# Four graph networks on 1,250 nodes: edge lists loaded ahead of x, rows moved as 120 and 5, last network's logits on TensorE and its residual inside the last head

## The reference

```python
hv = h.reshape(n, H, DIN)                       # H = 12, DIN = DOUT = 64
ft = jnp.einsum('nhd,od->nho', hv, W)
a1 = jnp.sum(ft * attn_l, axis=-1)
a2 = jnp.sum(ft * attn_r, axis=-1)
e = jax.nn.leaky_relu(a1[src] + a2[dst], negative_slope=0.2)
m = jax.ops.segment_max(e, dst, num_segments=n)
w = jnp.exp(e - m[dst])
alpha = w / jnp.maximum(segment_sum(w, dst)[dst], 1e-16)
agg = jax.ops.segment_sum(alpha[:, :, None] * ft[src], dst, num_segments=n)
res = jnp.einsum('nhd,od->nho', hv, W_res)
out = jax.nn.relu((agg + res).reshape(n, H * DOUT))
x = _layernorm(x + out, axis=-1)
```

## Time and profile before

| | us |
|---|---|
| three runs | 3564.36 (median), 3555.25, 3577.82 |
| the profiled execution | 3568.32 |
| its span, first to last instruction | 3566.5 |
| mean granted clock of TensorE | 0.944 of full |
| start to the end of the counting stage | 0 to 366 |
| first network | 366 to 1258 |
| second network | 1258 to 2770 |
| third network | 2770 to 2980 |
| last network: projections | 2980 to 3045 |
| last network: heads | 3045 to 3511 |
| tail and stores | 3511 to 3566.5 |

### The profile page before, as it was taken

How to read it: one execution, slowest core, us unless ns; L and a number is a source line. 1 busy time by engine, 2 the same in 40 slices (tenths; PEclk the granted TensorE clock), 3 DMA queues, 4 the chain that set the end, 5 groups by cost and what they waited for, 6 DMA issues and landing times. The chain is left out here.

```text
span 3566.5 us, 60526 instructions
## 1 busy us (share of the span) xinstructions
PE 3236.0 (91%) x20691; PEld 3023.4 (85%) x20691; DVE 2210.2 (62%) x4068; ACT 1338.6 (38%) x2524; POOL 930.8 (26%) x967
## 2 busy tenths in 40 slices
PE   3997997999998999999999899999989897899993
PEld 3886776888888999999988899999978585799993
DVE  3888736667677531118878401258868348888895
ACT  1145223333323121124546211134454212677782
POOL 1100733444445430014546200035555000000000
PEclk9988998999999999999999999999999798899896
DMA  2023433122111244247767433367766201000001
GB/s 78 23 79 94 141 112 107 55 97 90 58 61 62 92 129 129 90 142 244 240 207 241 151 113 101 100 202 241 238 202 191 89 22 72 1 1 1 0 1 44
DMA packets 157898, 386.93 MB, mean 108 GB/s; under 512 B 27083, under 2 KB 96248, under 8 KB 157673
## 3 DMA queue, kind: packets, MB, share of 16 engines
q0 software_dynamic: 47200, 173.39, 15.9%
q1 hardware_dynamic: 72989, 147.94, 11.9%
q10 hardware_dynamic: 37484, 62.75, 5.6%
HBM read 284.69 MB, written 99.32 MB: 108 GB/s over the span
## 5 line engine op out<-in xcount | busy, mean ns | idle before, releaser
L1832 PE MATMUL bank<-w_hi,xT_hi 128*125 128x384 f32 x1920 | 653.1, 340 | 8.0 <-ACT arena L1536 8.0
L1833 PE MATMUL bank<-w_lo,xT_hi 128*125 128x384 f32 x1920 | 650.9, 339 | 0.0
L1834 PE MATMUL bank<-w_hi,xT_lo 128*125 128x384 f32 x1920 | 650.8, 339 | 0.0
L1536 ACT COPY arena<-bank 125x384 f32<-125x384 f32 x320 | 153.6, 480 | 800.1 <-PE bank L1834 746.1
L817 POOL DMA_INDIRECT arena<-y_early,edges x204 | 233.9, 1146 | 817.3 <-issue 362.8
L891 DVE SCALAR_TENSOR_TENSOR row_lo<-arena,edges,row_hi 128x768 fp32r<-128x768 f32 x300 | 304.1, 1014 | 120.9 <-ACT row_hi L860 81.4
L2299 DVE CAST w_hi<-w_raw 128x2304 fp32r<-128x2304 f32 x35 | 47.6, 1359 | 531.4 <-PE bank L1834 525.5
L1832 PEld LDWEIGHTS bank<-w_hi,xT_hi 128*125 128x125 f32 x1920 | 358.3, 187 | 8.9 <-DVE w_lo L2300 4.7
L1833 PEld LDWEIGHTS bank<-w_lo,xT_hi 128*125 128x125 f32 x1920 | 358.3, 187 | 0.1
L1834 PEld LDWEIGHTS bank<-w_hi,xT_lo 128*125 128x125 f32 x1920 | 358.0, 186 | 0.1
L730 ACT ACTIVATE arena<-arena,low 125x1250 f32<-125x1250 f32 x170 | 227.7, 1339 | 345.0 <-DVE low L742 344.3
(11 more groups left out here) (351 smaller groups left out, 6628.7 us busy)
## 6 DMA issues: line engine op xcount, KB each, us to landing
y_early<-arena SPq DMA_DIRECT2D x200, 187.5 KB
w_raw<-in_L_gnn_W_dram ACTq DMA_DIRECT2D x30, 1152.0 KB, 7.4
arena<-own_mask_d SPq DMA_DIRECT2D x50, 610.4 KB
y_late<-arena SPq DMA_DIRECT2D x120, 187.5 KB
h_d<-arena ACTq DMA_DIRECT2D x40, 250.0 KB
arena<-in_L_gnn_W_dram SPq DMA_DIRECT2D x5, 1536.0 KB, 10.6
arena<-h_d ACTq DMA_DIRECT2D x30, 250.0 KB
wadj_d<-arena SPq DMA_DIRECT2D x10, 625.0 KB
```

Of the source, the lines that this page charges most:

```text
L1832: pe.matmul(b, xT_hi[:, k, v], w_hi[:, h, k], start=(k == 0), stop=False)
L1833: pe.matmul(b, xT_hi[:, k, v], w_lo[:, h, k], start=False, stop=False)
L1834: ins = pe.matmul(b, xT_lo[:, k, v], w_hi[:, h, k], start=False, stop=(k == KD - 1))
```

## The change

It has four parts. SP issues the twelve edge loads first and the load of x behind them. Loads and stores with 125 rows outermost are issued in two pieces, rows 0 to 119 and rows 120 to 124 (ROWS): the load of x, load_h, load_mask, the mask of the last network and the output stores; waits on their semaphores count two DMAs. Other transfers of 125 rows keep their form. In the last network's projection stage the attention vectors are laid out by chunk of 128 input columns (att3, 24 columns), multiplied once by the weights into logit3, and TensorE then computes logits with a 4-column matmul beside each 256-column one, all into bank 7, from which VectorE copies them to al3 at the end; its products and reductions go. In the last head, VectorE adds the residual and takes the statistics of a tile as soon as the tile's last head is in, computes the moments of the first seven tiles (ENDS = NT - 3) behind unit 16 of the pair, and normalises them behind unit 17; the last three follow after the last unit. ScalarE's square root is split the same way.

```diff
+        att3 = cut(at, KD, 2, 2)
+        logit3 = cut(at + 4 * KD, KD, 2, 2)
+        ENDS = NT - 3
...
+        ROWS = ((0, P - P % 15), (P - P % 15, P))
...
-            sp.dma_start(node_a, a["x"].rearrange("(n p) d -> p n d", p=P)).then_inc(bulk_loaded, 16)
-
             sp.wait_ge(rows_ready, 1)
             for i, v in enumerate([a["dst"], a["src"], a["edge_type_8"], a["edge_weight"]]):
...
+            for lo, hi in ROWS:
+                sp.dma_start(node_a[lo:hi], a["x"].rearrange("(n p) d -> p n d", p=P)[lo:hi]).then_inc(bulk_loaded, 16)
...
             def load_h(h):
-                sp.dma_start(h_raw[h % 2], h_d[h].rearrange("(n p) c -> p n c", p=P)).then_inc(h_loaded, 16)
+                for lo, hi in ROWS:
+                    sp.dma_start(h_raw[h % 2][lo:hi], h_d[h].rearrange("(n p) c -> p n c", p=P)[lo:hi]).then_inc(h_loaded, 16)
...
-                sp.dma_start(mask_slot[u % 2], own_mask_d[u % NT * P:(u % NT + 1) * P, :]).then_inc(mask_in[u % 2], 16)
+                for lo, hi in ROWS:
+                    sp.dma_start(mask_slot[u % 2][lo:hi], own_mask_d[u % NT * P + lo:u % NT * P + hi, :]).then_inc(mask_in[u % 2], 16)
...
-            sp.dma_start(att3[:, 0], spread(a["L3_gnn_attn_l"][0].rearrange("h c -> (h c)"), P)).then_inc(w3_loaded, 16)
-            sp.dma_start(att3[:, 1], spread(a["L3_gnn_attn_r"][0].rearrange("h c -> (h c)"), P)).then_inc(w3_loaded, 16)
-            sp.wait_ge(w3_cleared, 1)
+            sp.wait_ge(w3_cleared, 2)
+            for i, v in enumerate((a["L3_gnn_attn_l"], a["L3_gnn_attn_r"])):
+                for q in range(2):
+                    sp.dma_start(att3[q * C3:(q + 1) * C3, :, i, q], v[0].rearrange("(k q) c -> q c k", q=2)[q],
+                                 allow_slow_non_contiguous=True).then_inc(w3_loaded, 16)
...
-            sp.dma_start(mask, mask_d.rearrange("(n p) s -> p n s", p=P)).then_inc(mask_loaded, 16)
+            for lo, hi in ROWS:
+                sp.dma_start(mask[lo:hi], mask_d.rearrange("(n p) s -> p n s", p=P)[lo:hi]).then_inc(mask_loaded, 16)
...
-                sp.dma_start(out[d * P:(d + 1) * P, :], node_b[:, d]).then_inc(x_saved[d % 2], 16)
+                for (lo, hi), stored in zip(ROWS, x_saved):
+                    sp.dma_start(out[d * P + lo:d * P + hi, :], node_b[lo:hi, d]).then_inc(stored, 16)
...
+            act.copy(logit3.rearrange("p k i q -> p (k i q)"), bank[7][:, 0:4 * KD]).then_inc(w3T_ready, 1)
             act.copy(w3T.rearrange("p a b -> p (a b)"), bank[6][:, 0:256]).then_inc(w3T_ready, 1)
...
+                    if last and k == PAIR - 3:
+                        act_sqrt(act, "sqrt_act", rstd[:, 0:ENDS])
...
+            pe.matmul(bank[7][:, 0:4 * KD], w3[:, 0], att3.rearrange("p k i q -> p (k i q)"), start=True, stop=True).then_inc(w3_turned, 1)
+            pe.wait_ge(w3T_ready, 2)
...
                     for c in range(2):
-                        ins = pe.matmul(bank[q % 6][0:P, c * 256:(c + 1) * 256], xT[:, 2 * g + c, n * P:(n + 1) * P],
+                        k = 2 * g + c
+                        pe.matmul(bank[7][0:P, 4 * (n * KD + k):4 * (n * KD + k + 1)], xT[:, k, n * P:(n + 1) * P],
+                                  logit3[:, k].rearrange("p i q -> p (i q)"), start=True, stop=True)
+                        ins = pe.matmul(bank[q % 6][0:P, c * 256:(c + 1) * 256], xT[:, k, n * P:(n + 1) * P],
...
-                dve.wait_ge(f_taken, 3 * (n + 1))
-                for i in range(2):
-                    chain(dve.tensor_tensor(scratch3, node_a[:, n], att3[:, i], op=ALU.mult))
-                    chain(dve.tensor_reduce(al3[:, i, n], scratch3.rearrange("p (h c) -> p h c", c=C3), axis=AX_X, op=ALU.add))
+            for i in range(2):
+                chain.mark(dve.tensor_copy(al3[:, i].rearrange("p n (k q) -> p n k q", q=2),
+                                           bank[7][0:P, 0:4 * KD * NT].rearrange("p (n k i q) -> p n k i q", n=NT, k=KD, i=2)[:, :, :, i]))
...
+                    if last and q:
+                        dve.wait_ge(agg_taken, unit(u + k))
+                        chain(dve.scalar_tensor_tensor(node_b[:, d], res3[:, d], 0.0, node_b[:, d], op0=ALU.max, op1=ALU.add))
+                        dve_stats(dve, chain, node_b, d)
+                        if d == ENDS - 1:
+                            dve_moments(dve, chain, range(ENDS))
+                        if d == ENDS:
+                            dve_scale(dve, chain, node_b, node_b, range(ENDS))
```

More of the change, by code:

```diff
@@ L348, in build @@
         al3 = cut(rest + NT * N + node, 2, NT, H3, parts=P)
-        att3 = cut(rest + NT * N + node + 2 * NT * H3, 2, D, parts=P)
+        at = rest + NT * N + node + 2 * NT * H3
+        att3 = cut(at, KD, 2, 2)
+        logit3 = cut(at + 4 * KD, KD, 2, 2)
+        ENDS = NT - 3
         w3 = cut(rest + NT * N + node + 2 * NT * H3 + 2 * D, 2, 128)
         w3T = cut(rest + NT * N + node + 2 * NT * H3 + 2 * D + 256, 2, 128)
-        scratch3 = cut(rest + NT * N + node + 2 * NT * H3 + 2 * D + 512, D, parts=P)
         s_row3 = cut(rest + NT * N + node + 2 * NT * H3, 2, N, parts=P)
@@ L1153, in _ @@
                 sp.wait_ge(ln_done, 3 * NT + d + 1)
-                sp.dma_start(out[d * P:(d + 1) * P, :], node_b[:, d]).then_inc(x_saved[d % 2], 16)
-            for i in range(2):
-                sp.wait_ge(x_saved[i], 16 * NT)
+                for (lo, hi), stored in zip(ROWS, x_saved):
+                    sp.dma_start(out[d * P + lo:d * P + hi, :], node_b[lo:hi, d]).then_inc(stored, 16)
+            for stored in x_saved:
+                sp.wait_ge(stored, 16 * NT // 2 + 16 * NT)
         @block.gpsimd
@@ L1342, in _ @@
             next_phase(pool)
+            pool.memset(att3, 0.0).then_inc(w3_cleared, 1)
             pool.memset(w3, 0.0).then_inc(w3_cleared, 1)
@@ L1642, in _ @@
             act_pair(H3 // 2 - 1, True)
[L1643 removed]
+            act_sqrt(act, "sqrt_act", rstd[:, ENDS:NT])
         @block.tensor
@@ L2376, in _ @@
             next_phase(dve)
-            dve.wait_ge(bulk_loaded, 16 * 7)
+            dve.wait_ge(bulk_loaded, 16 * 8)
             for n in range(NT):
@@ L2425, in _ @@
             next_phase(dve)
-            dve.wait_ge(bulk_loaded, 16 * 9)
+            dve.wait_ge(bulk_loaded, 16 * 10)
             for n in range(NT):
@@ L2445, in _ @@
                                     bank[q % 6][0:P, :].rearrange("p (c i f) -> p c i f", c=2, i=2)[:, :, 0]).then_inc(f_taken, 1)
-                dve.wait_ge(f_taken, 3 * (n + 1))
-                for i in range(2):
-                    chain(dve.tensor_tensor(scratch3, node_a[:, n], att3[:, i], op=ALU.mult))
-                    chain(dve.tensor_reduce(al3[:, i, n], scratch3.rearrange("p (h c) -> p h c", c=C3), axis=AX_X, op=ALU.add))
+            for i in range(2):
+                chain.mark(dve.tensor_copy(al3[:, i].rearrange("p n (k q) -> p n k q", q=2),
+                                           bank[7][0:P, 0:4 * KD * NT].rearrange("p (n k i q) -> p n k i q", n=NT, k=KD, i=2)[:, :, :, i]))
             next_phase(dve)
-            dve.wait_ge(mask_loaded, 16)
+            dve.wait_ge(mask_loaded, 32)
             chain(dve.tensor_scalar(al3[:, 1], al3[:, 1], SLOPE - 1.0, None, op0=ALU.mult))
@@ L2507, in _ @@
             dve_pair(H3 // 2 - 1, True)
-            dve.wait_ge(agg_taken, unit((H0 + 1 + H3) * NT - 1))
-            for d in range(NT):
-                chain.mark(dve.scalar_tensor_tensor(node_b[:, d], res3[:, d], 0.0, node_b[:, d], op0=ALU.max, op1=ALU.add))
-            chain.wait()
-            for d in range(NT):
-                dve_stats(dve, chain, node_b, d)
-            dve_norm(dve, chain, node_b, node_b)
+            dve_moments(dve, chain, range(ENDS, NT))
+            dve_scale(dve, chain, node_b, node_b, range(ENDS, NT))
 _INS = ['x', 'src', 'dst', 'edge_type_8', 'edge_weight', 'L0_gnn_W1', 'L0_gnn_att_src1', 'L0_gnn_att_dst1', 'L0_gnn_b1',
```

20 lines of the change are left out of this document (8 added, 12 removed).

## The result

The changed kernel takes 3468.07 us (median of 4 runs, 3458.22 to 3472.38) against 3560.64 us (4 runs, 3555.25 to 3577.82) for the kernel before: a ratio of 0.9714, 95% interval 0.9676 to 0.9753. The two profiled executions, 3566.5 and 3470.6 us of span, lie 95.9 us apart. Each of the forecast's four terms came out about right, and the whole a quarter to a third larger than their sum.

What follows compares the result with a forecast made beforehand. TensorE, busy nine tenths of the span, was taken as the bound, so only its idle stretches could give: 26.5 + 9.7 + 13.3 + 27.5 = 77.0 us, from a median of 3564.4 to 3487 us, range 3466 to 3514.

Steps and rivals of the forecast that it cites:

- Part 3: Last network's projection stage, logits on TensorE: 40.9 us against 53.7, a matmul pair 0.64 us; gain 13.3 us.
- Part 1: Start of the kernel, edge lists issued ahead of x: lists in at 12.2 us; gain 26.5 us (22.4 to 29.7).
- x is in by 23 to 31 ... All hidden: Start: x, issued behind the edge lists, lands before the transposes want it at 33.5 us, so its load costs nothing.
- Part 2: First network's first attention units, rows as 120 and 5: first exp 6.6 us earlier, unit 2 3.1; together 9.7 (5 to 12).
- rival A: Split loads and stores: 120 rows move no faster than 125; total gain only 43 us, 3521; 8 in 100.
- Part 4: Last head and tail, residual and statistics within the head, stores in two pieces: gain 27.5 us (19 to 31).
- B: TensorE at half clock in reworked stretches: pairs 1.27 us, last head 6.6 a unit; total gain 30, 3534; 6 in 100.
- C: Slower: mask bursts on 15 engines lengthen GpSimd's scatter chain; 36 us slower needs 1.17 us more per trip; 2 in 100.

Runs made afterwards that it cites:

- b_logits: Kernel before with only the logits moved to TensorE, no filler waits, so the loop begins at 5192: 0.9897 (0.9869 to 0.9925) of the kernel before.
- b_logits_pad: Kernel before with only the logits moved to TensorE, plus 78 already met waits keeping the loop at 5231: 0.9967 (0.9927 to 1.0007).
- b_pad24: Kernel before plus 48 already met waits (24 instructions), so its loop begins at 5255: 0.9897 of the kernel before, median 3533.44 us.
- a_pad39: Changed kernel plus 78 already met waits (39 instructions), so its loop begins at 5231 again: 0.9772 of the kernel before, median 3496.49 us.
- a_same: Changed kernel run again with no edit: 0.9709 (0.9669 to 0.9749) of the kernel before, median 3462.15 us.
- a_rows125: Changed kernel with its split loads and stores as one piece of 125 rows again: 0.9838 of the kernel before, median 3499.21 us.
- b_resid: Kernel before with only the residual, statistics and first seven normalisations moved within the last head, stores whole: 0.9988 (0.9958 to 1.0017).
- a_xalone: Changed kernel with SP issuing the first weight load and attention loads only once x has landed: 0.9701 (0.9675 to 0.9728) of the kernel before.

## Why the prediction missed

**The sum left out a term.** It went through four stretches that the change touches and took the stages between at nothing. The step that failed is Part 3's "Removed: 20 products and 20 reductions, 39 us of VectorE": it priced their time and not their place in the code. Taking 39 instructions away moved the loop behind them into three blocks, worth 25 us in the times (b_logits against b_logits_pad: 0.0070 of 3565), 37 (b_pad24), 22 (a_pad39 against a_same) and 26 to 40 in the head stages of the profiles. The view that would have shown it was at hand before the run: the trace of before has four "issue" waits of 2.4 us at L736, 76 to 83 us apart, in the stage ahead of the one studied. The prediction read neither the head stage's waits nor its windows from 3100 to 3500.

With the stall put back (a_pad39), the four parts give 0.9772 (0.974 to 0.9804), 3483 on the 3564.36 us of the forecast, 3472 to 3494: the forecast of 3487 lies within. The sum was right for what it summed.

**Part 1, 26.5 forecast.** 24.7 measured. The cast came at 9.09, 3 earlier than taken. "x is in by 23 to 31 ... All hidden" is what failed: x lands at 35.2, and the prediction's own line, that it is wrong if x holds the transposes, applies. They were ready at 30.3, so x took 4.9 us of a gain of 29.6; that 24.7 is so near 26.5 is two errors against each other. The rate was the cause: taken as 210 to 381 GB/s (three times 127), it is 211 falling to 112 together with the loads behind it, and alone 206 falling to 147. A packet of x, 3 KB, takes 252 ns on average instead of 136 in the kernel before, so that three times the engines move these rows about 1.5 times as fast, not three times.

**Part 2, 9.7.** The first exp moved 6.8 and unit 2's mask 2.3 more (33.5 earlier at L740 where unit 1's was 31.2), 9.1, of which 6.6 is left 500 us on (L656 and L660 last run in one form at 1093.3 and 1062.3). But in five of the seven profiles of kernels with whole rows the distance from the last projection to the first L750 is 16.1 to 16.2 us, not the 13.2 of the profile read, so that this part may as well be worth 9.8 on the first exp alone. That 120 rows spread wider was right; rival A is refuted by the DMA share, and by a_rows125.

**Part 3, 13.3.** A pair takes 0.65 (0.64 forecast). The stage lasts 42.5, and 40.8 in a_same (2954.59 to 2995.38; 40.9 forecast). From the last transposes to the first L788 it gained 11.1 in this pair of profiles and 12.8 in most. (The 40 operations removed are 38.2 us by the earlier trace rows, not 39; no sum uses it.)

**Part 4, 27.5.** 39.6 less 11.9 is 27.7, and 25.4 against the four other profiles with the old end (102.3 less 76.9). Last mask 11.9 later (11.5), then 23.9 to the end (23.4), 5.5 behind the last normalisation (5 to 6). The split stores carry 16 (a_rows125) and the residual 8 to 11 (b_resid).

**Rivals.** B, half clock in the reworked stretches, took 3.4 us of the projection stage in the changed kernel's profile. It took 34 us of it in one of the ten profiles that have the new stage (a_xalone, where a pair then takes 1.27 us, as B has it) and 14 in another (a_pad39), so it costs up to 17 us at times. In the last head it did happen: the clock is 0.50 from 3427.1 to 3437.3 and again from 3444.1, for all the work that is left. But B's price there, 6.6 us a unit, is refuted: at either clock VectorE's masks follow each other in 5.4 us, as in the sum, since VectorE is the bound. C: from the first L750 to the last transposes before the projection stage all kernels took 2438 to 2455 us, with whole mask rows and with rows in two pieces alike (means 2444.4 and 2445.3), so bursts of mask rows cost GpSimd's chain nothing that arrives. The -4.6 of the table is within that.

## To carry to other kernels

Before a sum is made, list the idle time that the profile puts down to "issue" at the first instruction of each loop body, on every engine, with the clock of the windows behind it: here four stalls of 2.5 us stood for 30. An edit that changes the number of instructions ahead of a loop is an edit to that loop: count its body and where it begins, and try a few instructions of filler, since 24 of them gained 37 us on a kernel that was otherwise left alone. Compare variants of one kernel only at the same placement, or the placement is measured with them.

## What the runs showed of the hardware

- VectorE's code comes in packets of 8 KB on q14, each asked for as VectorE enters the block of 128 instructions ahead of it (packets behind 21, 152 and 273 instructions of a pass that enters blocks behind 17, 145 and 273). A loop of 290 instructions is fetched again in each pass when it begins 100, 111 or 127 into a block of 128, and not at all when it begins 7, 8, 72 or 88 in. A back edge with a fetch stalls VectorE for 2.4 to 2.8 us, and for 4.6 to 4.8 at 127, where two packets follow each other.
- TensorE's wait at such an edge, 1.94 us at the first of the kernel before, is followed by a clock of 0.50 for 3 to 34 us, at 23 of 24 edges in six profiles. In the kernel before the longest spell is behind the third edge: three windows of 8 us from 3293 to 3317 at 0.51, 0.50 and 0.50, though TensorE was busy throughout. The longest of all is in a_pad39, from 3175.9 to 3210.0. The length differs from edge to edge, and no run tells why.
- In the projection stage the clock fell to 0.50 for 34 us in a_xalone, under continuous matmuls, and for none in a_same, with the same instructions there. Executions of one kernel, where there are three or more, spread over 9 to 61 us, and in the four runs of the changed kernel the mean granted clock goes with the time (0.964 at 3458.22, 0.957 at 3464.96, 0.954 at 3471.18, 0.951 at 3472.38). That such spells are all of the spread is not shown.
- The load of x as 120 + 5 rows moves at 188 to 206 GB/s alone until its end nears, and the output stores at 238 to 280 GB/s (windows of 5 us in four profiles, the last one of each left out), against 126 to 131 for 125 rows. The gain over five engines was about 1.5 for the load and 1.8 to 2.2 for the stores.
